# Moving the projection pieces behind the value product in two fused attentions

## The reference, cut to what matters

```python
xm = _modulate(_ln(x), sh_msa, sc_msa)
q = (xm @ Wq + bq).reshape(B, S, NH, DH)
k = (xm @ Wk + bk).reshape(B, S, NH, DH)
v = (xm @ Wv + bv).reshape(B, S, NH, DH)
q = q / DH
w = jnp.einsum('bqhc,bkhc->bhqk', q, k)
w = jax.nn.softmax(w, axis=-1)
y = jnp.einsum('bhqk,bkhc->bqhc', w, v).reshape(B, S, H)
x = x + g_msa[:, None, :] * (y @ Wo + bo)
...
# second attention, before the scores
q = q * cos + rotate_half(q) * sin
k = k * cos + rotate_half(k) * sin
```

## Time and profile before

| | |
|---|---|
| median of 3 runs | 953.08 us (949.27 to 955.69) |
| profiled execution | 950.83 us, its span 949.0 us |
| TensorE busy | 896.8 us, 95% of the span |
| VectorE busy | 583.5 us, 61% |
| ScalarE busy | 521.6 us, 55% |
| GpSimd busy | 463.6 us, 49% |
| mean granted TensorE clock | 0.982 of full speed |

### The profile page before, as it was taken

The page is one execution under the profiler, slowest core; times in us unless marked ns, Lnnn a source line. Parts: engine busy times, 40 slices in busy tenths (PEclk is TensorE's granted clock), DMA queues, the critical chain, the costliest instruction groups (busy, mean ns, idle before and its releaser), DMA issues.

```text
span 949.0 us, 14600 instructions
## 1 busy us (share of the span) xinstructions
PE 896.8 (95%) x5256; PEld 540.0 (57%) x5256; DVE 583.5 (61%) x916; ACT 521.6 (55%) x952; POOL 463.6 (49%) x634
## 2 busy tenths in 40 slices
PE   5999999999989999999999998999999999999997
PEld 3454344343347779777878764343443433687874
DVE  4787878888764464553423387577778785234323
ACT  2147776777764444335454532577677777644331
POOL 4386343606566536447544328782751016565430
PEclk9899999999999899999999999799999999999999
DMA  7577757463111130141232137465574421100001
GB/s 225 155 223 208 197 150 213 127 178 103 48 47 35 55 125 1 46 147 47 95 117 91 23 109 200 123 181 158 134 205 125 102 81 47 47 13 1 23 23 45
DMA packets 67375, 101.32 MB, mean 107 GB/s; under 512 B 22236, under 2 KB 33576, under 8 KB 66920
## 3 DMA queue, kind: packets, MB, share of 16 engines
q1 hardware_dynamic: 53624, 77.44, 27.4%
q0 software_dynamic: 11104, 20.36, 8.2%
q10 hardware_dynamic: 2576, 2.59, 1.0%
HBM read 64.65 MB, written 35.02 MB: 105 GB/s over the span
## 4 chain that ended last, share of the span: by engine, by line
PE 78%; DVE 8%; ACT 5%; issue 4%; POOL 3%; DMA 2%; ACTq 0%; DVEq 0%; POOLq 0%
PE PS L688 13%; PE PS L656 12%; PE PS L1091 12%; PE PS L1073 12%; PE PS L611 7%; PE PS L602 7%; PE PS L667 4%; ACT PH L748 3%; DVE U L844 2%; PE PS L447 2%; PE PS L624 2%; PE PS L1206 1%; PE PS L1194 1%; DVE st L393 1%; POOL PHR L1138 1%
## 5 line engine op out<-in xcount | busy, mean ns | idle before, releaser
L844 DVE TENSOR_REDUCE U<-PS 128x2 f32<-128x1024 f32 x256 | 308.5, 1219 | 62.4 <-PE PS L667 61.3
L748 ACT ACTIVATE PH<-PS 128x512 f32<-128x512 f32 x512 | 277.6, 598 | 96.6 <-PE PS L656 93.3
L656 PE MATMUL PS<-UR 50*128 50x512 f32 x512 | 195.7, 453 | 7.9 <-ACT PH L748 5.8
L667 PE MATMUL PS<-UR 48*128 48x512 f32 x512 | 191.9, 471 | 8.1 <-DVE U L844 5.7
L1138 POOL TENSOR_TENSOR PHR<-PH,PHR 128x512 fp32r<-128x512 f32 x96 | 128.8, 1346 | 118.7 <-ACT PHR L1128 118.7
L656 PEld LDWEIGHTS PS<-UR 50*128 50x128 f32 x512 | 82.2, 186 | 162.8 <-ACT PH L748 105.7
L1091 PE MATMUL PS<-UR,PHR 128*128 128x256 f32 x768 | 158.9, 290 | 4.3 <-POOL PHR L1138 3.2
L688 PE MATMUL PS<-PH,U 128*32 128x512 f32 x1024 | 137.1, 608 | 0.0
L1091 PEld LDWEIGHTS PS<-UR,PHR 128*128 128x128 f32 x768 | 124.7, 189 | 21.8 <-issue 16.4
L1091 PE MATMUL PS<-W2R,PHR 128*128 128x256 f32 x384 | 108.2, 282 | 0.0
L1127 ACT ACTIVATE PH<-PS,col 128x512 f32<-128x512 f32 x64 | 44.0, 687 | 103.4 <-PE PS L1073 103.4
(11 more groups left out here) (241 smaller groups left out, 1267.8 us busy)
## 6 DMA issues: line engine op xcount, KB each, us to landing
UR<-d_parts SPq DMA_DIRECT2D x112, 192.0 KB, 4.1
d_parts<-UR POOLq DMA_DIRECT2D x76, 256.0 KB, 5.2
d_o<-U SPq DMA_DIRECT2D x32, 256.0 KB, 2.1
U<-in_L_cond_W_dram SPq DMA_DIRECT2D x8, 1024.0 KB, 7.8
W<-in_L_cond_W_dram SPq DMA_DIRECT2D x24, 256.0 KB, 3.1
U<-d_o SPq DMA_DIRECT2D x32, 128.0 KB
U<-d_rec SPq DMA_DIRECT2D x16, 256.0 KB
gates<-d_gate SPq DMA_DIRECT2D x3, 1024.0 KB, 7.0
```

The costliest lines, as they stand in the source:

```text
L656: self.close(pe.matmul(dst, KP[g // 2][r:r + SROWS + 2, j, kt * P:(kt + 1) * P], QP[g // 2][r:r + SROWS + 2, j, :], start=True, stop=True) ...
L667: ins = pe.matmul(bank(2 + (w + 2) % 4), QP[g // 2][r:r + SROWS, j, qt * P:(qt + 1) * P], KP[g // 2][r:r + SROWS, j, :], start=True, stop= ...
L748: nc.scalar.activation(PH[:, m % 2, j, :], self.where("ST", n), ACT.Exp).then_inc(self.a_free, 1)
L844: v.tensor_reduce(mx[:, G % 2, :].rearrange("p (r c) -> p r c", r=2)[:, :, c // 2], PS[:, 2 + (w + 1) % 4:4 + (w + 1) % 4, :], AX.X, ALU.m ...
```

## The change

All tasks named here move by whole steps; none is added or taken away. The pieces of Q and K of batches 1 to 3, and all pieces of V and PJ, go from 4k+2 to 4k+4, which is the first step of the next four: there they stand right behind PV (which ends step 4k+3) and ahead of the four's first ST. For "S" and "W" the number is written relative to the last piece, so they move by two as well; "R" moves by one (its distance goes from 5 to 4) and stands in the same step as a piece. M, T, O, FILL and all others keep their steps. Batch 0's Q and K keep theirs.

```diff
-                    at = -80 + 5 * q + part if first else -30 + 4 * (2 * q + part) if b == 1 else o - 62 + 4 * (2 * q + part)
+                    at = -80 + 5 * q + part if first else -28 + 4 * (2 * q + part) if b == 1 else o - 60 + 4 * (2 * q + part)
                     put(at, c, b, 2 * half + part)
                 if rope:
-                    put(at + (1 if first else 5), "R" + c, b, half)
+                    put(at + (1 if first else 4), "R" + c, b, half)
                 put(at + (2 if first else 7 if rope else 4), "S" + c, b, half)
                 put((-67, -59 if rope else -34)[half] if first else at + 14, "W" + c, b, half)
...
-            put(-18 + 4 * t if first else o + 34 + 4 * t, "V", b, t)
-            put(64 * b + 114 + 4 * t, "PJ", b, t)
+            put(-16 + 4 * t if first else o + 36 + 4 * t, "V", b, t)
+            put(64 * b + 116 + 4 * t, "PJ", b, t)
```

## The result

The changed kernel takes 971.67 us (median of 4 executions, 966.02 to 976.87) against 951.17 for the kernel before (4 executions), a ratio of 1.0222 with the interval 1.0171 to 1.0273. The forecast was 975, range 965 to 984. The profiled execution has a span of 969.1 us, 20.1 more than before. All ratios and intervals in this text leave out slow executions, of which there were two, 972.41 and 1308.61 us, both of the kernel with only Q and K moved.

The account below looks back on a forecast made before the run. TensorE, 78% of the chain, was taken to bound the kernel. Terms 21.6 + 0.6 - 1.9 + 3.4 - 1.4 - 0.1 = +22.2 us gave 973.0 for the profiled execution, 975 us by the median, range 965 to 984.

Parts of the forecast that it names:

- The bound and the latency: Attentions: TensorE sets the time; with three banks the fourth ST waits for the first exponential, 0.54 + 0.61 + 0.04 us.
- The term per four: Fours with a piece in the middle, 80 in all: 3.68 against 3.40 us, taken as 0.27 each, +21.6 us.
- M fours: 14 fours with M and a piece: +0.31 us each, 0.04 above the term already counted, +0.6 us.
- T fours: Fours 0 and 16 of each attention, where transposition T also stands in: -0.5 us each below the term, -1.9 us.
- O behind a piece: Seven fours where O waits for ScalarE's eviction of a piece, delaying the first exponential: 0.49 us each, +3.4 us.
- R: Eight R of batches 2 and 3, no longer splitting two pairs: about 1.06 us each instead of 1.24, -1.4 us.
- The end of the first attention: Fours 60 to 63: S5F starts earlier, last pieces wait for its last part; +1.0 instead of 1.1, so -0.1 us.
- The steps ahead of step 0: Steps -34 to -1, without STs, where VectorE's maxima set the pace: zero, bounds -2 and +2 us.
- The first: Rival: the piece's time pays for the fourth ST's wait; -0.19 x 80 = -15 us, 938 us; chance 0.06.
- The second rival: Loss in pairs is real but the attentions give it back through vanished waits or half clock; 950 to 962 us; chance 0.05.
- The third, slower still by the clock: Rival: waits make the granted clock fall to 1.2 GHz in two more stretches, costing 10 us; 985 us; chance 0.09.
- The sum: Whole kernel: 21.6 + 0.6 - 1.9 + 3.4 - 1.4 - 0.1 = +22.2 us.

Follow-up runs that it names:

- the cut kernels: Exponentials of 128 of 512 columns from each attention's third four on: changed kernel 940.77 us, ratio 0.988; kernel before 943.04 us, ratio 0.9912.

## Why the prediction was right

*The bound and the latency.* Right. The chain of the earlier trace rows, read in fours that had no piece, is the chain of all fours now. The experiments hold it up: another user in the fourth place waits in the same way (1.18), a shorter exponential takes the loss away, and a piece that is the third use before a product makes it wait for the eviction, with M moved as well as with the pieces ahead of the second pair. No run gave the rotation a fourth bank, the direct test of the count.

*The term per four.* 0.27 forecast, 3.67 - 3.40 = 0.27 measured. M fours: 4.16 against 3.84, the 0.31 forecast. T fours: four 16 went from 5.14 to 4.92, -0.22 where -0.23 was forecast (0.27 - 0.5).

*O behind a piece.* Right mechanism, size 2.6 instead of 3.4: the fourth ST moved by 0.43 in the first attention and 0.34 in the second, where I took 0.49 for both (the fourth ST starts at 1.61 in the timeline above, not at 1.68).

*R.* Mis-sized: R ahead of a piece, in the timeline of the changed kernel:

```profile
611.80 1.13 PE L624 MATMUL PS<-U,rot 128*128 128x512 f32 x2
612.77 1.03 PE L602 MATMUL PS<-XN,WA 128*128 128x256 f32 x4
613.72 0.50 PE L656 MATMUL PS<-UR 50*128 50x512 f32 x1
```

R takes 0.97 and the piece 0.95 instead of 1.06, so R adds 0.86, not 1.06 (fours of 4.53 against 3.67). Where it had split two pairs without M it had added 1.24, beside M 0.97: 4 x -0.38 + 4 x -0.11 = -2.0, where -1.4 was forecast.

*The end of the first attention.* +1.0 forecast up to the next layer's first product, -0.5 measured. VectorE's S5F was ahead as forecast, and the waits came where I put them, but shorter than my starts and durations gave; the changed kernel's:

```profile
281.47 0.49 PE L656 MATMUL PS<-UR 50*128 50x512 f32 x1 [1.23 <-DVE tsc L817]
...
285.93 0.49 PE L656 MATMUL PS<-UR 50*128 50x512 f32 x1 [1.00 <-DVE tsc L817]
```

The last piece then ran in time in which TensorE had been idle before.

*The steps ahead of step 0.* Zero within 2 was too narrow: +3.4 and -2.8 in one profile. The -2.7 or -2.8 of the second attention is there in all four profiles with all pieces behind PV, and -2.1 with Q and K moved alone, so it belongs to the change; TensorE waits 1.4 us for VectorE's maxima there instead of 2.8. In the first attention TensorE had the full clock at the start this time, ran ahead, and waited for a transfer:

```profile
49.54 1.22 PE L667 MATMUL PS<-UR 48*128 48x512 f32 x3 [2.70 <-DMA UR<-d_parts]
```

In the two profiles of the kernel before the same product starts at about the same time, at 49.23 and 49.51 us, though TensorE had half clock from 38.2 to 48.5 and from 37.4 to 44.2. So half clock ahead of that transfer cost little, and half clock behind it is paid for: the changed kernel had it there, from 49.4 to 56.2 us, and took 14.8 us from this product to the first ST where both profiles of the kernel before took 11.5. Its own repeat had it from 50.5 to 57.3; with O first it ended at 50.5, and there the loss is +1.0 only. Why it falls behind the transfer in one execution and ahead of it in another is open.

*The rivals.* The first is refuted: the fourth ST waits, and a longer period doesn't pay for it. Its price was too high for what the cut kernels show (0.05 a four, with a rest of the wait in it, not 0.19). The Trainium skill says in "TensorEngine Tiling (Array Packing)", section Key Properties, that a change of tiling mode drains TensorE. The 0.05 agrees with that in direction, though a drain can't be told there from other fixed costs of a run; the PV cut, with more changes of mode and less time (2.48 against 2.62), shows that a drain isn't what bounds here. The second rival, that the attentions give it back elsewhere, holds in part: 8.8 us came back at -2.8, -2.9 and -3.1, and other stretches took as much. The third, slower still by the clock, looked true in the first profile (13.7 us at half clock, +5.2 us in fours 54 to 57), but the repeat had 3.4 us there and the kernel before had such a stretch elsewhere: it belongs to the execution.

*The sum.* +22.2 forecast, +20.1 in the profile, +20.5 by the medians. What the forecast explains is the 19.8 us of the fours at full clock, for which its terms give some 20. That the whole time came as close is luck in part: the rest of the execution cancelled in this kernel, but not with O first, where the fours lose 17.1 us and the kernel 10 by the ratio, nor with V and PJ alone (12.3 and 20.6).

## What to carry to other kernels

Where several products share a short rotation of accumulation banks, count the uses from one product to the next on the same bank: between them lie the first product's latency and its whole reader, here 1.19 us, and a long product of another kind is worth most where it stands under that time. Before moving tasks next to one another, look for a place in the trace where they already are. Judge such moves by the length of a period at full clock; whole executions differ by several us for other reasons.

## What the runs showed of the hardware

- TensorE's granted clock fell to 1.2 GHz in stretches of 3.4 to 20 us (27 to 83 us per execution), in one execution and not in another. Within the stretch from 242 to 256 us in the repeat of the kernel before TensorE is busy all the time (13.99 of 14.00 us), but just before it stood still in part: it waited 0.48 and 0.60 us for maxima between 239.5 and 242.2 us and was busy 1.62 of 2.70 us. The first execution had the same waits there and kept the full clock. Windows of the repeat, then of the first execution (columns as the earlier trace rows):

```profile
239.50:242.20 2.70, 1.62 (x12) 0.78 (x8) 2.70 (x4) 1.55 (x4) 2.23 (x7) 1.00 0.33 111
```

```profile
239.50:242.20 2.70, 1.63 (x8) 0.59 (x7) 2.70 (x4) 1.68 (x3) 2.24 (x8) 1.00 0.30 103
```

- Where the third pair of a run had to wait for the eviction of a piece (0.47 us), the run took 1.07 us instead of the 0.91 that the starts of undisturbed pairs give. 0.10 of it is the distance from the waiting pair to what follows, 0.43 instead of 0.33. Why that distance grows behind a wait wasn't tried.
- The same value product in two halves takes 0.57 + 0.57 instead of 1.00 us.
